# Attention written out for all eight units, and GpSimd adding a tile of probabilities for four heads at once

## What is computed

```python
q = h @ wq / sqrt(512); k = h @ wk; v = h @ wv      # 16 heads of 32
q, k = rotary_pos_emb(q), rotary_pos_emb(k)
logits = einsum('bhik,bhjk->bhij', q, k)            # 2048 x 2048 for each of 2 x 16 heads
a = softmax(logits, axis=-1)
y = einsum('bhij,bhjv->bhiv', a, v)
x = x + y @ wo
...
```

## Time and profile before

| | |
|---|---|
| three runs, median (lowest to highest) | 3886.65 us (3883.5 to 3889.67) |
| the profiled execution, its own time | 3881.74 us |
| its span, first to last instruction | 3879.9 us |
| mean granted TensorE clock | 0.942 |
| PE busy | 3463.9 us, 89% |
| POOL busy | 2111.9 us, 54% |
| attention's exponentials | from 431.5 to 2157.7 us |
| POOL's adds of probabilities, 1024 instructions | 1159.2 us and 165.2 us |

### The profile page before, as it was taken

How to read it: one execution, slowest core, us unless ns; L and a number is a source line. 1 busy time by engine, 2 the same in 40 slices (tenths; PEclk the granted TensorE clock), 3 DMA queues, 4 the chain that set the end, 5 groups by cost and what they waited for, 6 DMA issues and landing times. The chain is left out here.

```text
span 3879.9 us, 47864 instructions
## 1 busy us (share of the span) xinstructions
PE 3463.9 (89%) x16544; PEld 2271.6 (59%) x16544; DVE 2037.3 (53%) x3268; ACT 1529.4 (39%) x2795; POOL 2111.9 (54%) x1675
## 2 busy tenths in 40 slices
PE   7997899989999899989999456699979996999997
PEld 5775445544554445544554145588858884777776
DVE  5764777767777677767775155111111113344443
ACT  2331466656666566656666222211111112121121
POOL 2654378876879688886988412122212223454553
PEclk9998999999999899999999777799989997999999
DMA  5556677858686677858655555211011103221220
GB/s 188 173 158 169 123 145 131 154 103 148 131 149 137 110 147 133 157 109 143 135 115 115 135 186 192 92 44 44 33 55 44 44 33 126 78 79 58 86 76 37
DMA packets 146742, 438.11 MB, mean 113 GB/s; under 512 B 15936, under 2 KB 16448, under 8 KB 120384
## 3 DMA queue, kind: packets, MB, share of 16 engines
q1 hardware_dynamic: 123456, 267.22, 25.7%
q0 software_dynamic: 23040, 167.78, 22.4%
HBM read 171.49 MB, written 95.42 MB: 69 GB/s over the span
## 5 line engine op out<-in xcount | busy, mean ns | idle before, releaser
L680 DVE TENSOR_REDUCE part_max<-ps_att 128x1 f32<-128x512 f32 x1972 | 1228.5, 684 | 432.5 <-PE ps_att L601 432.1
L723 ACT ACTIVATE probs<-ps_att 128x512 f32<-128x512 f32 x2048 | 1064.8, 603 | 522.2 <-PE ps_att L575 461.5
L774 POOL TENSOR_TENSOR prob_sums<-prob_sums,probs 128x512 f32<-128x512 f32 x896 | 1159.2, 1568 | 24.5 <-DMA probs<-probs 24.5
L575 PE MATMUL ps_att<-q_stack,k_stack 97*128 97x512 f32 x2048 | 873.1, 429 | 40.9 <-PEq L53 24.2
L601 PE MATMUL ps_att<-k_stack,q_stack 96*128 96x512 f32 x1972 | 788.6, 400 | 0.0
L575 PEld LDWEIGHTS ps_att<-q_stack,k_stack 97*128 97x128 f32 x2048 | 392.1, 192 | 532.0 <-ACT probs L723 359.9
L623 PE MATMUL ps_att<-probs,v_tok 128*32 128x512 f32 x4096 | 548.1, 607 | 0.0
L1362 POOL TENSOR_TENSOR ml_g_lo<-ml_g,ml_g_hi 128x512 fp32r<-128x512 f32 x128 | 164.8, 1288 | 653.5 <-DVE ml_g_hi L1338 653.5
L601 PEld LDWEIGHTS ps_att<-k_stack,q_stack 96*128 96x128 f32 x1972 | 380.7, 193 | 68.1
L1338 DVE CAST ml_g_hi<-ml_g 128x512 fp32r<-128x512 f32 x128 | 54.7, 427 | 570.0 <-ACT ml_g L1296 570.0
L756 POOL DMA_DIRECT2D probs<-probs x160 | 152.9, 956 | 307.6 <-PE ps_att L623 301.4
(11 more groups left out here) (186 smaller groups left out, 4803.7 us busy)
## 6 DMA issues: line engine op xcount, KB each, us to landing
probs<-probs POOLq DMA_DIRECT2D x160, 1024.0 KB, 8.5
q_stack<-qk SPq DMA_DIRECT2D x186, 128.0 KB, 7.1
k_stack<-qk SPq DMA_DIRECT2D x42, 512.0 KB, 11.4
qk<-rot_hi SPq DMA_DIRECT2D x64, 256.0 KB, 3.4
qk<-rot_lo SPq DMA_DIRECT2D x64, 256.0 KB, 2.6
av_gate_rows<-gate SPq DMA_DIRECT2D x64, 256.0 KB
x_in_sb<-in_x SPq DMA_DIRECT2D x8, 1024.0 KB, 8.8
v<-v_stage SPq DMA_DIRECT2D x8, 1024.0 KB, 5.1
```

Of the source, the lines that this page charges most:

```text
L575: nc.tensor.matmul(sT[u % 3], t["kS"][0:S3 + 1, b, h, k * P:(k + 1) * P], t["qS"][0:S3 + 1, h, n * TB:(n + 1) * TB], start=True, stop=True)\
L680: nc.vector.tensor_reduce(t["pm"][:, r, k:k + 1], mx[mx_uses % 3], AX.X, ALU.max)\
L723: nc.scalar.activation(t["p"][:, at % PR, h, :], sT[(at * G + h) % 3], ACT.Exp)\
L774: nc.gpsimd.tensor_tensor(x, first, t["p"][:, w % PR, h, :], ALU.add).then_inc(s["acc_done"], 1)
```

## The change

It does two things. The hardware loop and the separate last pass are replaced by one pass over 8 units, written out: `attend_groups` becomes `attend`, `plan` makes one list of 512 steps, and the semaphores are cleared once and count through. And each round of `add_round` becomes one instruction over all four heads, 128x2048, that waits for the exponentials of all four and is counted once; ACT waits for it before the first head's exponential.

```diff
-POOL_ADDS = G * len(POOL_ROUNDS)
+POOL_ADDS = len(POOL_ROUNDS)
...
-def plan(halves, nexts):
+def plan():
...
-    for half, b in enumerate(halves):
+    for unit in range(UNITS):
+        b = unit % B
...
-    def added(w, h):
+    def added(w):
...
-        return w // LT * POOL_ADDS + G * r + h + 1
+        return w // LT * POOL_ADDS + r + 1
...
-                        if v % LT not in PE_SUMS:
-                            act.wait_ge(s["acc_done"], added(v, h))
-                        elif h == 0:
+                        if v % LT not in PE_SUMS and h == 0:
+                            act.wait_ge(s["acc_done"], added(v))
+                        if v % LT in PE_SUMS and h == 0:
                             act.wait_ge(s["psum"], summed(v))
...
-                for h in range(G):
-                    pool.wait_ge(s["exp"], w * G + h + 1)
-                    x = t["acc"][:, n % 2, h, :]
-                    if r == 0:
-                        if n >= 2:
-                            pool.wait_ge(s["sum_done"], n - 1)
-                        first = t["p"][:, POOL_FIRST % PR, h, :]
-                    else:
-                        pool.wait_ge(s["acc_done"], n * POOL_ADDS + G * (r - 1) + h + 1)
-                        first = x
-                    nc.gpsimd.tensor_tensor(x, first, t["p"][:, w % PR, h, :], ALU.add).then_inc(s["acc_done"], 1)
+                pool.wait_ge(s["exp"], G * (w + 1))
+                x = t["acc"][:, n % 2]
+                if r == 0:
+                    if n >= 2:
+                        pool.wait_ge(s["sum_done"], n - 1)
+                    first = t["p"][:, POOL_FIRST % PR]
+                else:
+                    pool.wait_ge(s["acc_done"], n * POOL_ADDS + r)
+                    first = x
+                nc.gpsimd.tensor_tensor(x, first, t["p"][:, w % PR], ALU.add).then_inc(s["acc_done"], 1)
...
-        with nc.Fori(0, NG - 1) as g:
-            attend_groups(nc, c, a, g, s, t, ps)
-        attend_groups(nc, c, a, NG - 1, s, t, ps, nexts=(True, False))
+        attend(nc, c, a, s, t, ps)
```

More of the change, by code:

```diff
@@ L43 @@
 STEPS = NB * LT
+UNITS = NG * B
 JOBS = G * TT
@@ L521, in _ @@
                     load_q(g, b, NB - 1)
-                if nexts[st["half"]]:
+                if unit + 1 < UNITS:
                     if w in K_AT or w in V_AT:
@@ L554, in _ @@
                     store_sums(at // LT - 1)
[L555 to L559 removed]
+            store_values(blocks - 1)
+            store_sums(blocks - 1)
+            sp.wait_ge(s["y_stored"], 16 * blocks)
+            sp.wait_ge(s["l_stored"], 16 * blocks)
             for name, count in loaded.items():
@@ L579, in wait_stacks @@
             def wait_stacks(st):
-                half = st["half"]
+                unit = st["unit"]
                 b, j = st["job"]
@@ L614, in values @@
                 n, k = w // LT, w % LT
-                half = steps[w]["half"]
+                unit = steps[w]["unit"]
                 pe.wait_ge(s["exp"], G * (w + 1))
@@ L618, in values @@
                     pe.wait_ge(s["o_kept"], n)
-                if half and w % STEPS == 0:
-                    pe.wait_ge(s["v_in"], 32 * half)
+                if unit and w % STEPS == 0:
+                    pe.wait_ge(s["v_in"], 32 * unit)
                 for h in range(G):
```

49 lines of the change are left out of this document (22 added, 27 removed).

## The result

The changed kernel takes 3906.86 us (3904.25 to 3912.55, 4 runs), the kernel before beside it 3885.07: a ratio of 1.0056, 95% interval 1.0039 to 1.0074. It is **slower by some 22 us** where 3838 was forecast. Its profiled execution took 3908.17 us, of which 3906.4 are its span, at a mean granted clock of 0.944.

The account below looks back on a forecast made before the run. PE was taken to set attention's pace, with POOL and the DMAs close behind. The terms -60.4 - 2 + 15 - 4 + 3 = -48.4 us took the median 3886.65 to 3838 us, range 3815 to 3862.

Parts of the forecast that it names:

- The change of passes is removed: -60.4 us: Between passes: the three drained changes become ordinary crossings of units, saving 21.03, 21.29 and 18.10 us, together 60.4.
- the crossing of units: Where a pass's first unit meets its second: the window 646.93 to 698.58 takes 51.65 us, so it costs nothing.
- the backward branch: At the loop's end between passes: worth about 3 us each, by instruction fetch, all of it inside the 60.4.
- Shorter on POOL: POOL's rounds: one add of 128x2048 makes a round 4.7 us against 4.97, gaining nothing in a steady block.
- rival (a): Second blocks: POOL issues accumulating transfers earlier and the delays dissolve, -70 us, 3816 us; chance 0.22.
- Rival (c): POOL's rounds in attention: the long add really takes 6.6 us and POOL becomes the bound, 3964 us; chance 0.03.
- Later for ACT: +15 us: Seven second blocks of units: ACT's first exponential waits for the whole round, making PE 2.15 us later in each.
- Fewer cold starts: -4 us: Second blocks of three first units: they now begin like second units and lose less; half of 7.8 us taken.
- -2 us at attention's end: PE's last sums at attention's end: the last five rounds they wait for get shorter, -2 us.
- The clock: +3 us: PE in another block or two: stalls in one piece drop it to its lower clock, +3 us, bounds 0 and 9.
- 0.95 for "faster": Whole kernel: the chance given to a measurement faster by more than 0.2%, 7.8 us; within 0.02, slower 0.03.

Follow-up runs that it names:

- experiment one: The changed kernel, written out, but with four adds of 128x512 a round and ACT's wait for each head: 3825.81 us, ratio 0.9854.
- the long pause: The changed kernel with a 128x512 memset of a scratch tile on POOL ahead of tile 12's transfer: 3833.56 us, ratio 0.9867.
- the spread loads: experiment one with the next unit's K loads at steps 2, 6, 10, 22, 26, 38 and V loads at 42, 54: 3798.69 us, ratio 0.9779.

## Why the prediction was wrong

- **"The change of passes is removed: -60.4 us": right.** The window from a pass's last `o_sb` and the one ahead of it took 124.3, 124.5 and 121.3 us at the three changes and take 103.4, 103.5 and 103.6 in experiment one, the change without the whole-tile round: 59.7 us less. The window that I called the crossing of units, 646.93 to 698.58, is the first block of the second unit; the crossing lies in the window before it, from 595.17, which takes 51.76 us, so it costs 0.1 and the reading holds. From the first to the last `o_sb` experiment one gains 46.5 us, the rest having been taken back in second blocks (below). That the whole kernel gains 59 again is chance: in the two profiled executions some 9 us lie ahead of the first `o_sb` or behind the last, of which the runs tell nothing. As to the backward branch, PE's idle time behind the barrier is 7.58, 7.87 and, where nothing goes back, 4.36 us; the size fits, but no run tests the branch or the fetch of instructions by itself.
- **"Shorter on POOL": the size right, the conclusion wrong, and this is the step that failed.** I had 4.7 us a round; a lone add takes 4.57, two in a row 9.62. From that I wrote "nothing in a steady block", since POOL isn't the bound. But POOL also issues transfers, and rounds stand ahead of one of them in its program. The text even said that POOL "issues its accumulating transfers earlier", as a gain, in rival (a), and asked of no queue what the earlier transfer would be put ahead of. The end of its issue moved from 2.50 to 1.86 us behind the first small transfer, over an edge near 2.25, and the stall that it made cost 73 us: the difference between the changed kernel and the one with the long pause. Two rounds of 0.27 us saved each, as I had them, give 0.54 of these 0.64 us, so the numbers for it were there. No rival had it. Rival (c) named steady blocks above 51.7 us, but for an add of 6.6 us.
- **"Later for ACT: +15 us": the wait alone costs 15 us with four adds, 8 with the changed kernel's own instruction.** With four adds the size is the forecast one by chance: only 6.4 of the 15 us lie in second blocks, where the working had them all. The prediction that only second blocks would show it holds for the changed kernel's instruction (its second blocks lose 42.2 against 34.9, and the steady ones nothing), where it is 7 us for 15. In the kernel after itself little of this is seen (its second blocks at 1156.84 and 1822.41 take 51.60), probably since PE's stall ahead of them gives POOL the time.
- **"Fewer cold starts: -4 us": the wrong sign.** The seven second blocks lose 34.9 us in experiment one against 20.8 before. They are not a matter of how a pass starts but of when transfers meet, as the spread loads show, which take nearly all of it away. Why they lose more written out than with the loop no run shows.
- **"-2 us at attention's end": right in size.** PE waits 10.0 us there for POOL's last round, where it was 11.8; the last window between evictions is 44.3 us against 43.8.
- **"The clock: +3 us": mis-sized, by the stall.** A stalled block shows 0.94, and its PE is busy for 54.6 us where it was 51.65: 3 us of the 6 that it loses. The eighteen windows of 56 us or more hold 45 us of this, and PE's waits for `max_turned` are 67.7 us in all.

Without the collision the total would have stood, if not every term of it: 3833.56 us with the long pause, 3838 forecast. In part that is luck. The second blocks of that kernel lose 42.2 us where they lost 20.8, 21 us more and not the 11 of +15 and -4. Its profiled execution (3844.10 us, the slowest of four) gains only 38.4 us from the first to the last `o_sb`, and where the rest of the median's gain of 52 lies that trace doesn't show. The forecast was right on the change of passes and on the length of an add. 0.95 for "faster" was far too sure with a path to PE, the small transfers, that had 1.5 us of slack (6.36 - 4.9) and had not been read.

## What to carry to other kernels

An engine that issues transfers moves them whenever its other work gets shorter, even where it is idle most of the time and nobody waits for it. For each transfer that moves, read what else goes out within some us of it, who waits for that and with how much slack: here 2 KB waited behind 1 MB. Compare the ends of the issuing rows, not their starts: here the starts told half of the move. And a small transfer that PE depends on is best issued well ahead of a large one or held apart by a semaphore, not left to a distance that happens to fit.

## What the runs showed of the hardware

- Four 2 KB transfers issued by SP 0.6 us apart land, counted from the first issue, in 3.5 us if a 1 MB transfer issued by POOL keeps away. They land in 4.8 to 5.0 if POOL's issue ends 2.45 to 2.6 us after the first small one, in 5.4 to 6.0 at 2.3, in 7 to 8 at 2.1 and in 8 to 9.7 at 1.85. One to seven waves of its 8 KB packets then stand ahead of the last small transfer's packets of 512 bytes.
- The first packet of POOL's transfer starts 0.56 to 0.59 us behind the end of the issuing row, with either form of the adds ahead of it. The start of that row can lie 0.3 us inside the add before it.
- PE's stall of 3.2 us is followed by 6.6 us at a granted clock of 0.50, and so costs about twice its length.
- POOL's back-to-back adds: four of 128x512 come 4.97 us apart as a round, one of 128x2048 takes 4.57 to 4.9 us, so one instruction for four saves 0.1 to 0.4 us. Two such rounds bring the issue behind them 0.64 us forward by its end.
- DVE's reductions of PSUM don't feel the longer POOL instruction: 684 ns each before and 683 after.
